# x1 of the next sample ahead of the end of an older norm on VectorE, in a chain of conditioned residual layers

## The chip, the cores and the metric

The kernel runs on one core of one Trainium2 chip. The metric is the device time of the whole program in microseconds (us). Before the change three runs took 1144.47, 1144.3 and 1142.27 us; the median is 1144.3.

The engines are called as in the profile: PE is TensorE's matmuls and PEld its weight loads, DVE is VectorE, ACT is ScalarE, POOL is GpSimd, SP is the engine that issues most DMAs.

## What is computed

The input x holds 128 samples of 128 rows by 512 features, fp32. Each sample runs through four residual layers, each with weights or factors that belong to a category of that sample:

```python
def reference(x, itok_B_0_7, condB_deltat, itok_B_0_63, itok_B_0_8, ...):
    # layer 0: W = weight[subject_id]; y = einsum('bnh,boh->bno', x, W) + bias[subject_id]
    x = x + _L0_cond_ref(x, itok_B_0_7, L0_cond_weight, L0_cond_bias)
    # layer 1: pairs of rows are rotated and scaled by angles and amplitudes ** delta_t
    x = x + _L1_cond_ref(x, condB_deltat, L1_cond_amplitudes, L1_cond_frequencies)
    # layer 2: einsum('bsd,bdh->bsh', x, W[cat_ids]) + b[cat_ids]
    x = x + _L2_cond_ref(x, itok_B_0_63, L2_cond_W, L2_cond_b)
    # layer 3: adapter (512 -> 128 -> relu -> 512), added to its input, then a norm
    #   over the 512 features with gamma and beta of the sample's language
    x = x + _L3_cond_ref(x, itok_B_0_8, L3_cond_W1, ..., L3_cond_gamma, L3_cond_beta)
    return x
```

Layer 0 has 8 weight matrices for 128 samples, layer 2 has 64.

## The kernel before

The samples are handled one at a time, in an order sorted by subject, so that the weight of layer 0 (W0) changes seldom: after the first two samples at samples 30, 31, 61, 70, 89, 110 and 117. The weight of layer 2 (W2, 1 MB) is loaded anew for each sample. The residual of layers 0 and 2 is folded in by adding the identity to the diagonal blocks of the weight. The matmuls of layers 0 and 2 and the second one of the adapter run on operands split into a rounded part (hi) and its rest (lo), as hi x hi + lo x hi + hi x lo. ScalarE makes the hi parts; VectorE makes the lo parts of the weights and of x2; GpSimd makes the lo parts of x and h.

Each engine has its own program, written out by hand as a loop `for s in range(1, B)`; one pass is called a turn here. Semaphores alone tie the engines together, and each engine works through its list in order.

TensorE in turn s: the first half of layer 0 of sample s+1 (L1048, L1052), layer 2 of sample s (L1090 with x2T_hi and w_hi, L1094 with x2T_lo, L1100 with w_lo, the last two of its four matmuls waiting for the second half of w_lo), the rest of layer 0 of sample s+1 (L1059, L1064, then l0_done), the transpose of x3 (L1110), the adapter's second matmul of sample s-1 (up, L1130 to L1133, then up_done), the rotation of sample s+1 (L1075, needs x1), the adapter's first matmul of sample s (down, L1120).

VectorE in turn s, in this order: w_lo, first half (rest_of_w2, L873); x2T_lo (L890); a half or both halves of w0_lo where sample s+1 brings a new W0 (rest_of_w0, L864); w_lo, second half (L873); the mixing matrix (L845); centre of sample s-2, which subtracts the mean and multiplies by gamma (L924); x3 of sample s (finish_l2, L902, needs l2_done); the end of the norm of sample s-2 (finish_norm, L935: times rstd, plus x3_beta, into the output buffer yb); x1 of sample s+1 (finish_l0, L883: ps_l0 plus bias, needs l0_done); the first half of w0_lo where sample s+2 brings a new W0 and 18 <= s+2 < 110 (rest_of_w0, L864); the add of x3 to the adapter's result of sample s-1 (add_x3, L915, needs up_done).

GpSimd in turn s: var_eps and rstd of sample s-2 (L482, L487) after the second half of w_lo; the identity onto W2 of sample s+1 (L469); h_lo (L500); x_lo of sample s+2 (L476); x3_beta of sample s-1 (add_beta, L508); if sample s+3 brings a new W0, the identity onto it (L461) and the copy of its bias (L464).

SP in turn s issues the loads of W2 (s+3), x (s+4) and the rows per sample (s+2), then the store of sample s-2, which waits for out_made (L342), then the load of W1 (s+2), which waits for the down matmuls of turn s (L336), then perhaps a W0 (s+5).

The profile's names leave buffer numbers out: `ps_l` is ps_l0 or ps_l2, `x<-ps_l,b_sb` is x1, `x<-ps_l,rows` is x3, `x_beta` is x3_beta, `w_lo<-w_in,w_hi` is w2_lo at L873 and w0_lo at L864.

Of the kernel before, what the change touches and what calls it, by code (L numbers as in the profile page):

```python
# [18 lines left out]
def conditioned_residual_stack(  # L19
# [32 lines left out]
    with ctx:  # L52
# [199 lines left out]
        def is_first(eng, s):  # L252
            return eng.value_load(ids[0:1, bass.ds(4 * B + s, 1)], min_val=0, max_val=1)
# [12 lines left out]
        def landed(s, n):  # L266

            return 16 * (s // n + 1)
# [448 lines left out]
        def _(dve):  # L717
# [112 lines left out]
            def coefficients():  # L830

                dve.wait_ge(power_made, 4)
                dve.wait_ge(trig_made, 1)
                for n, wide in enumerate((sin_of, cos_of)):
                    dve.tensor_tensor(wide.rearrange("p (f e) -> p f e", e=2),
                                      power.unsqueeze(2).broadcast_to([P, F, 2]),
                                      trig[:, n * F:(n + 1) * F].unsqueeze(2).broadcast_to([P, F, 2]), ALU.mult)\
                        .then_inc(coef_wide, 1)

            def make_mix(s):  # L840

                if s >= 1:
                    dve.wait_ge(mix_done, s)
                dve.wait_ge(diag_made, s + 1)
                dve.scalar_tensor_tensor(out=mix[:, :], in0=signed_swap[:, :], scalar=sin1[:, s:s + 1],  # L845
                                         in1=ps_diag[:, :], op0=ALU.mult, op1=ALU.add).then_inc(mix_made, 1)
# [8 lines left out]
            def rest_of_w0(s, parts, first):  # L855

                e = s % 2
                with dve.If(first):

                    dve.wait_ge(w2_hi_made, 2 * s - 1)  # L860
                    dve.wait_ge(l0_done, s - 1)
                    for n in parts:
                        half = halves[n]
                        dve.tensor_tensor(w0_lo[e][:, half], w0_in[e][:, half], w0_hi[e][:, half].bitcast(fp32),  # L864
                                          ALU.subtract).then_inc(w0_lo_made[e], 1)

            def rest_of_w2(s, n):

                half = halves[n]
                if s >= 1:  # L870
                    dve.wait_ge(l2_done, s)
                dve.wait_ge(w2_hi_made, 2 * s + n + 1)
                dve.tensor_tensor(w2_lo[:, half], w2_in[s % WB][:, half], w2_hi[:, half].bitcast(fp32),  # L873
                                  ALU.subtract).then_inc(w2_lo_made, 1)

            def finish_l0(s):

                if s >= 1:
                    dve.wait_ge(mix_done, s)
                if s < 2:  # L880
                    dve.wait_ge(b0_loaded[s], 16)
                dve.wait_ge(l0_done, s + 1)
                dve.tensor_tensor(x1[:, :], ps_l0[:, :], b0_sb[s % 2][:, :], ALU.add).then_inc(x1_made, 1)  # L883

            def rest_of_x2T(s):

                if s >= 1:
                    dve.wait_ge(l2_done, s)
                dve.wait_ge(x2T_hi_made, s + 1)
                dve.tensor_tensor(x2T_lo[:, :], ps_mix[:, :], x2T_hi[:, :].bitcast(fp32), ALU.subtract)\  # L890
                    .then_inc(x2T_lo_made, 1)

            def finish_l2(s):

                dve.wait_ge(l2_done, s + 1)
                if s >= 2:
                    dve.wait_ge(x3beta_made, s - 1)
                if s < 2:
                    dve.tensor_copy(x3[s % X3B][:, :], ps_l2[:, :]).then_inc(x3_made, 1)
                    return  # L900
                dve.wait_ge(rows_loaded[s % RB], landed(s, RB))
                dve.tensor_tensor(x3[s % X3B][:, :], ps_l2[:, :], rows[s % RB][:, bias_of], ALU.add).then_inc(x3_made, 1)  # L902

            def rest_of_wup(n):

                dve.wait_ge(wup_hi_made, n + 1)
                dve.tensor_tensor(wup_lo[:, wup_parts[n]], wup_sb[:, wup_parts[n]],
                                  wup_hi[:, wup_parts[n]].bitcast(fp32), ALU.subtract).then_inc(wup_lo_made, 1)

            def add_x3(s):  # L910
                y = ps_y[s % 2]
                dve.wait_ge(up_done, s + 1)
                if s >= 1:
                    dve.wait_ge(mean_made, s)
                dve.scalar_tensor_tensor(out=y[:, :], in0=y[:, :], scalar=1.0, in1=x3[s % X3B][:, :],  # L915
                                         op0=ALU.mult, op1=ALU.add, accum_out=y_sum[:, :]).then_inc(y_made, 1)

            def centre(s):

                y = ps_y[s % 2]  # L920
                if s < 2:
                    dve.wait_ge(rows_loaded[s], 16)
                dve.wait_ge(squares_made, s + 1)
                dve.scalar_tensor_tensor(out=y[:, :], in0=y[:, :], scalar=neg_mean[:, 0:1],  # L924
                                         in1=rows[s % RB][:, gamma_of],
                                         op0=ALU.add, op1=ALU.mult).then_inc(scaled_made, 1)

            def finish_norm(s):

                if s >= OB:  # L930
                    dve.wait_ge(out_stored[s % OB], landed(s, OB) - 16)
                dve.wait_ge(x3beta_made, s + 1)
                dve.wait_ge(scaled_made, s + 1)
                dve.wait_ge(rstd_made, s + 1)
                dve.scalar_tensor_tensor(out=yb[s % OB][:, :], in0=ps_y[s % 2][:, :], scalar=rstd[:, 0:1],  # L935
                                         in1=x3_beta[s % 2][:, :], op0=ALU.mult, op1=ALU.add).then_inc(out_made, 1)
# [27 lines left out]
            def in_two_turns(s):  # L964

                return 18 <= s < 110

            for s in range(1, B):
                rest_of_w2(s, 0)
                rest_of_x2T(s)  # L970
                if s < LAST:
                    rest_of_w0(s + 1, (1,) if in_two_turns(s + 1) else (0, 1), first)
                rest_of_w2(s, 1)
                if s == 1:
                    coefficients()
                    rest_of_wup(0)
                    finish_l2(1)
                    dve.wait_ge(coef_sorted, 1)
                    dve.tensor_scalar(cos1[:, 2:B], ps_y[1][:, 2:B], 1.0, None, ALU.add).then_inc(coef_made, 1)
                    rest_of_wup(1)  # L980
                    finish_l0(2)
                    rest_of_wup(2)
                    dve.wait_ge(coef_made, 2)
                if s < LAST:
                    make_mix(s + 1)
                first = is_first(dve, s + 2) if s < LAST - 1 else None
                if s >= 2:
                    centre(s - 2)
                if s >= 2:
                    finish_l2(s)  # L990
                    finish_norm(s - 2)
                    if s < LAST:
                        finish_l0(s + 1)
                if in_two_turns(s + 2):
                    rest_of_w0(s + 2, (0,), first)
                add_x3(s - 1)
# [220 lines left out]
```

## Time and profile before

| | before |
|---|---|
| median of three runs | 1144.3 us |
| the profiled execution | 1143.54 us |
| its span, first to last instruction | 1141.1 us |
| mean granted TensorE clock | 0.992 of full speed |
| PE busy | 1102.6 us (97%) |
| DVE busy | 916.4 us (80%) |
| ACT busy | 778.7 us (68%) |
| POOL busy | 677.9 us (59%) |
| DMA | 353.50 MB, mean 310 GB/s |

How to read it: the span is the time in which instructions ran; the program's own time is longer by what lies around it (2.4 us here). Busy times overlap, since the engines work side by side. A busy share near 100% says that an engine bounds the kernel only if its work is also on the chain that ended last; the chain and the waits show that. In the timelines each row has the start in us from the beginning of the span, the duration in us, the engine, the line, the operation and its tiles, and how many instructions were merged; in brackets stands how long the engine was idle before it and what ended that.

### The profile page before, as it was taken

What the parts mean: (1) busy time and instruction counts of PE and PEld (TensorE: products, weight loads), DVE (VectorE), ACT (ScalarE), POOL (GpSimd) and SP (SyncE); (2) the same over time, 40 slices, a digit from 0 to 9 for tenths busy, and PEclk for the clock granted to TensorE, in tenths of its full rate; (3) what the DMA queues carried; (4) which work ended last, traced back from release to release, by engine and by line L of the source; (5) the groups of instructions that cost most, each with busy time, mean ns of one, the idle gap of its engine ahead of it and who ended that gap; (6) DMA issues with size and microseconds to landing.
All of it is one profiled execution on the core that took longest, in us unless ns stands there. A gap on an engine that the chain in (4) does not pass through costs nothing.

```text
span 1141.1 us, 28378 instructions
## 1 busy us (share of the span) xinstructions
PE 1102.6 (97%) x6046; PEld 924.0 (81%) x6046; DVE 916.4 (80%) x1373; ACT 778.7 (68%) x1824; POOL 677.9 (59%) x807
## 2 busy tenths in 40 slices
PE   4799999999999999999999999999999999999996
PEld 2588888888788888888888888887888888787885
DVE  7787787778987787778978877878877878888876
ACT  3476776767676776767767666767767767676764
POOL 5756556557755656556656556566556566565563
PEclk9899999999999999999999999999999999999999
DMA  7898979897998999799989889988998999798882
GB/s 247 307 330 302 321 284 334 315 309 277 381 338 295 322 316 315 269 351 327 333 303 361 307 275 341 323 300 308 356 310 286 342 316 356 263 369 323 312 297 70
DMA packets 97554, 353.50 MB, mean 310 GB/s; under 512 B 11870, under 2 KB 12510, under 8 KB 79932
## 3 DMA queue, kind: packets, MB, share of 16 engines
q1 hardware_dynamic: 95756, 350.39, 86.7%
q14 instruction: 162, 1.33, 0.3%
q8 instruction: 52, 0.85, 0.3%
q10 hardware_dynamic: 1584, 0.93, 0.3%
HBM read 316.94 MB, written 34.34 MB: 308 GB/s over the span
## 4 chain that ended last, share of the span: by engine, by line
PE 92%; DVE 2%; issue 2%; ACT 1%; DMA 1%; POOL 1%; DVEq 0%; SPq 0%; POOLq 0%; ACTq 0%
PE ps_mix L1075 10%; PE ps_l L1064 10%; PE ps_l L1100 10%; PE ps_l L1048 10%; PE ps_l L1094 10%; PE ps_l L1090 10%; PE ps_hT L1120 9%; PE ps_l L1059 5%; PE ps_x3T L1110 5%; PE ps_l L1052 5%; PE ps_y L1133 3%; PE ps_y L1131 3%; PE ps_y L1130 3%; DVE w_lo L873 1%; DMA x_in<-xT 1%
## 5 line engine op out<-in xcount | busy, mean ns | idle before, releaser
L595 ACT ACTIVATE w_hi<-w_in 128x1024 fp32r<-128x1024 f32 x256 | 270.8, 1058 | 219.5 <-POOL w_in L469 219.5
L873 DVE TENSOR_TENSOR w_lo<-w_in,w_hi 128x1024 fp32r<-128x1024 f32 x256 | 333.7, 1303 | 19.8 <-ACT w_hi L595 18.1
L482 POOL TENSOR_SCALAR var_eps<-square_sum 128x1 f32<-128x1 f32 x128 | 24.4, 191 | 414.5 <-DVE w_lo L873 307.9
L902 DVE TENSOR_TENSOR x<-ps_l,rows 128x512 f32<-128x512 f32 x126 | 87.0, 691 | 124.3 <-PE ps_l L1100 124.3
L640 ACT ACTIVATE x3T<-ps_x3T,minus_bup 128x128 f32<-128x128 f32 x512 | 145.8, 366 | 49.3 <-PE ps_x3T L1110 48.0
L508 POOL TENSOR_TENSOR x_beta<-x,rows 128x512 f32<-128x512 f32 x128 | 168.8, 1319 | 0.0
L476 POOL TENSOR_TENSOR x_lo<-x_in,x_hi 128x512 fp32r<-128x512 f32 x127 | 164.1, 1292 | 7.5 <-ACT x_hi L571 7.5
L469 POOL TENSOR_TENSOR w_in<-w_in,ident 128x512 f32<-128x512 f32 x128 | 166.5, 1301 | 2.9 <-DMA w_in<-W 2.9
L1075 PEld LDWEIGHTS ps_mix<-mix,x 128*128 128x128 f32 x1024 | 125.0, 192 | 32.9 <-issue 32.8
L1048 PE MATMUL ps_l<-w_hi,x_hi 128*128 128x512 f32 x512 | 150.2, 415 | 0.0
L1075 PE MATMUL ps_mix<-mix,x 128*128 128x128 f32 x1024 | 141.9, 282 | 4.9 <-DVE x L883 4.9
L1100 PE MATMUL ps_l<-w_lo,x2T_hi 128*128 128x512 f32 x512 | 138.9, 391 | 5.7 <-DVE w_lo L873 5.7
L1090 PE MATMUL ps_l<-w_hi,x2T_hi 128*128 128x512 f32 x512 | 139.4, 394 | 0.2 <-ACT w_hi L595 0.2
L1094 PE MATMUL ps_l<-w_hi,x2T_lo 128*128 128x512 f32 x512 | 138.3, 393 | 0.3 <-DVE x2T_lo L890 0.3
L1064 PE MATMUL ps_l<-w_lo,x_hi 128*128 128x512 f32 x512 | 137.4, 391 | 0.0
L1120 PE MATMUL ps_hT<-x3T,w_in 128*128 128x128 f32 x1024 | 135.4, 276 | 0.0
L915 DVE SCALAR_TENSOR_TENSOR ps_y<-ps_y,x 128x512 f32<-128x512 f32 x128 | 89.5, 699 | 47.6 <-PE ps_y L1133 47.6
L1120 PEld LDWEIGHTS ps_hT<-x3T,w_in 128*128 128x128 f32 x1024 | 124.8, 192 | 0.4 <-issue 0.4
L1100 PEld LDWEIGHTS ps_l<-w_lo,x2T_hi 128*128 128x128 f32 x512 | 95.8, 188 | 28.3 <-DVE w_lo L873 8.8
L1090 PEld LDWEIGHTS ps_l<-w_hi,x2T_hi 128*128 128x128 f32 x512 | 96.7, 189 | 22.6 <-issue 1.5
L1094 PEld LDWEIGHTS ps_l<-w_hi,x2T_lo 128*128 128x128 f32 x512 | 96.4, 189 | 22.1 <-DVE x2T_lo L890 2.3
L1064 PEld LDWEIGHTS ps_l<-w_lo,x_hi 128*128 128x128 f32 x512 | 96.2, 188 | 20.0
(148 smaller groups left out, 1843.7 us busy)
## 6 DMA issues: line engine op xcount, KB each, us to landing
w_in<-W SPq DMA_DIRECT2D x128, 1024.0 KB, 6.6
rows<-sample_rows SPq DMA_DIRECT2D x128, 768.0 KB, 7.1
x_in<-xT SPq DMA_DIRECT2D x128, 256.0 KB, 6.2
w_in<-W SPq DMA_DIRECT2D x128, 256.0 KB, 5.0
out<-yb SPq DMA_DIRECT2D x128, 256.0 KB, 6.6
w_in<-W0T SPq DMA_DIRECT2D x7, 1024.0 KB, 5.5
wup_sb<-Wup SPq DMA_DIRECT2D x1, 2560.0 KB, 13.7
w_in<-W0T SPq DMA_DIRECT2D x4, 512.0 KB, 6.4
```

Of the source, the lines that this page charges most:

```text
L469: pool.tensor_tensor(diagonal_of(w2_in[s % WB]), diagonal_of(w2_in[s % WB]), ident[:, :].unsqueeze(1).broadcast_to([P, C, P]), ALU.add).th ...
L476: pool.tensor_tensor(x_lo[s % 2][:, :], x_in[s % XB][:, :], x_hi[s % 2][:, :].bitcast(fp32), ALU.subtract).then_inc(x_lo_made, 1)
L508: pool.tensor_tensor(x3_beta[s % 2][:, :], x3[s % X3B][:, :], rows[s % RB][:, beta_of], ALU.add)\
L595: act.activation(w2_hi[:, halves[n]], w2_in[s % WB][:, halves[n]], ACT.Copy).then_inc(w2_hi_made, 1)
L873: dve.tensor_tensor(w2_lo[:, half], w2_in[s % WB][:, half], w2_hi[:, half].bitcast(fp32), ALU.subtract).then_inc(w2_lo_made, 1)
L1048: pe.matmul(ps_l0[:, :], x_hi[s % 2][:, c * N:(c + 1) * N], w0_hi[s % 2][:, c * D:(c + 1) * D], start=(c == 0), stop=False)
L1064: mm = pe.matmul(ps_l0[:, :], x_hi[s % 2][:, c * N:(c + 1) * N], w0_lo[s % 2][:, c * D:(c + 1) * D], start=False, stop=(c == C - 1))
L1075: mm = pe.matmul(ps_mix[:, c * N:(c + 1) * N], x1[:, c * P:(c + 1) * P], mix[:, :], start=True, stop=True)
L1090: pe.matmul(ps_l2[:, :], x2T_hi[:, c * N:(c + 1) * N], w2_hi[:, c * D:(c + 1) * D], start=(s >= 2 and c == 0), stop=False)
L1094: mm = pe.matmul(ps_l2[:, :], x2T_lo[:, c * N:(c + 1) * N], w2_hi[:, c * D:(c + 1) * D], start=False, stop=False)
L1100: mm = pe.matmul(ps_l2[:, :], x2T_hi[:, c * N:(c + 1) * N], w2_lo[:, c * D:(c + 1) * D], start=False, stop=(c == C - 1))
L1120: mm = pe.matmul(ps_hT[:, :], w1_in[s % 2][:, c * A:(c + 1) * A], x3T[:, c * N:(c + 1) * N], start=(c == 0), stop=(c == C - 1))
```

## The change

In VectorE's turn, finish_l0(s + 1) is moved ahead of finish_norm(s - 2). The two operations themselves, their waits and all other programs stay as they are. The order x3, end of norm, x1 becomes x3, x1, end of norm. It concerns turns 2 to 126. The rows per sample (bias, gamma and beta in one load) and rstd first on GpSimd belong to the kernel before already.

```diff
@@ -988,9 +988,9 @@
                     centre(s - 2)
                 if s >= 2:
                     finish_l2(s)
-                    finish_norm(s - 2)
                     if s < LAST:
                         finish_l0(s + 1)
+                    finish_norm(s - 2)
                 if in_two_turns(s + 2):
                     rest_of_w0(s + 2, (0,), first)
                 add_x3(s - 1)
```

## Rows read from the trace of the kernel before

**Rows 1.** The page: the chain that ended last, shares of the span by engine
```profile
PE 92%; DVE 2%; issue 2%; ACT 1%; DMA 1%; POOL 1%; DVEq 0%; SPq 0%; POOLq 0%; ACTq 0%
```
**Rows 2.** Waits, whole span: engine line waited for, us in total, times, longest us
```profile
PE ps_mix L1075 <- DVE x L883: 4.9, 3, 3.7
```
**Rows 3.** Timeline of an ordinary turn: start us, us, engine, line, operation
```profile
607.95 1.07 PE L1064 MATMUL ps_l<-w_lo,x_hi 128*128 128x512 f32 x4
608.31 0.74 DVE L935 SCALAR_TENSOR_TENSOR yb<-ps_y,rstd,x_beta 128x512 f32<-128x512 f32 x1
...
609.13 0.69 DVE L883 TENSOR_TENSOR x<-ps_l,b_sb 128x512 f32<-128x512 f32 x1
...
610.20 0.70 DVE L915 SCALAR_TENSOR_TENSOR ps_y<-ps_y,x 128x512 f32<-128x512 f32 x1 [0.38 <-PE ps_y L1133]
...
610.82 1.22 DVE L873 TENSOR_TENSOR w_lo<-w_in,w_hi 128x1024 fp32r<-128x1024 f32 x1
...
611.96 0.68 DVE L890 TENSOR_TENSOR x2T_lo<-ps_mix,x2T_hi 128x512 fp32r<-128x512 f32 x1
...
612.85 1.23 DVE L873 TENSOR_TENSOR w_lo<-w_in,w_hi 128x1024 fp32r<-128x1024 f32 x1 [0.21 <-ACT w_hi L595]
...
614.13 1.07 PE L1094 MATMUL ps_l<-w_hi,x2T_lo 128*128 128x512 f32 x4
```
**Rows 4.** Timeline of the turn after a late TensorE (turn 88)
```profile
796.43 0.73 DVE L935 SCALAR_TENSOR_TENSOR yb<-ps_y,rstd,x_beta 128x512 f32<-128x512 f32 x1
796.56 1.08 PE L1064 MATMUL ps_l<-w_lo,x_hi 128*128 128x512 f32 x4
...
797.75 0.69 DVE L883 TENSOR_TENSOR x<-ps_l,b_sb 128x512 f32<-128x512 f32 x1 [0.58 <-PE ps_l L1064]
```
**Rows 5.** Timeline: x1 and SP's store and W1 load in an ordinary turn
```profile
848.35 0.69 DVE L883 TENSOR_TENSOR x<-ps_l,b_sb 128x512 f32<-128x512 f32 x1
...
848.83 0.35 SPq L342 DMA_DIRECT2D out<-yb  x1
...
851.38 0.33 SPq L336 DMA_DIRECT2D w_in<-W  x1
```
**Rows 6.** Timeline, turns 59 and 60, sample 61's W0; last row: turn 87, sample 89
```profile
548.59 1.28 POOL L476 TENSOR_TENSOR x_lo<-x_in,x_hi 128x512 fp32r<-128x512 f32 x1
...
549.33 1.63 DVE L864 TENSOR_TENSOR w_lo<-w_in,w_hi 128x1024 fp32r<-128x1024 f32 x1
...
549.83 2.27 POOL L508 TENSOR_TENSOR x_beta<-x,rows 128x512 f32<-128x512 f32 x1
...
551.49 1.70 DVE L873 TENSOR_TENSOR w_lo<-w_in,w_hi 128x1024 fp32r<-128x1024 f32 x1
...
556.10 0.73 PE L1100 MATMUL ps_l<-w_lo,x2T_hi 128*128 128x512 f32 x2 [0.60 <-DVE w_lo L873]
...
788.76 2.28 POOL L508 TENSOR_TENSOR x_beta<-x,rows 128x512 f32<-128x512 f32 x1
```
**Rows 7.** Timeline, turns 28 and 29: the W0 of sample 30, before sample 31's
```profile
284.42 2.29 POOL L508 TENSOR_TENSOR x_beta<-x,rows 128x512 f32<-128x512 f32 x1
286.67 2.28 POOL L461 TENSOR_TENSOR w_in<-w_in,ident 128x512 f32<-128x512 f32 x1
288.89 1.61 POOL L464 COPY b_sb<-b_in 128x512 f32<-128x512 f32 x1
...
289.95 1.62 DVE L873 TENSOR_TENSOR w_lo<-w_in,w_hi 128x1024 fp32r<-128x1024 f32 x1
```
**Rows 8.** Timeline, turn 29: the first half of the W0 of sample 31
```profile
294.03 0.69 DVE L883 TENSOR_TENSOR x<-ps_l,b_sb 128x512 f32<-128x512 f32 x1 [0.27 <-PE ps_l L1064]
294.94 1.62 DVE L864 TENSOR_TENSOR w_lo<-w_in,w_hi 128x1024 fp32r<-128x1024 f32 x1 [0.22 <-ACT w_hi L595]
...
295.43 2.28 POOL L508 TENSOR_TENSOR x_beta<-x,rows 128x512 f32<-128x512 f32 x1
```
**Rows 9.** Timeline, turn 109: the first w_lo ahead of sample 110's W0
```profile
968.09 1.88 DVE L873 TENSOR_TENSOR w_lo<-w_in,w_hi 128x1024 fp32r<-128x1024 f32 x1
```

## The prediction, made before the change was run

> **What bounds the kernel now.** I read the page first: the chain that ended last is TensorE for 92% of the span [rows 1]. So an edit on VectorE is worth only what it takes from, or adds to, TensorE's waits. The second view is the list of waits: in the whole run TensorE's matmuls waited on x1 (L883) three times, 4.9 us together, 3.7 of them once [rows 2]; that long one belongs to the start, which the change does not touch. The third view is the timeline of one ordinary turn [rows 3]. Its reader should compare two ends: the last L1064 matmul of the next sample ends at 607.95+1.07 = 609.02, the norm on VectorE at 608.31+0.74 = 609.05, and x1 starts at 609.13. Which of the two released x1? One turn decides it: there the norm ended at 796.43+0.73 = 797.16, the matmuls at 796.56+1.08 = 797.64, and x1 started at 797.75, 0.11 after the matmuls, the same 0.11 as in the ordinary turn, though the norm had been done for 0.59 us [rows 4]. So x1 already starts as early as TensorE lets it; the norm in front of it fills a gap in which VectorE has nothing else.
>
> I also use a spacing: VectorE starts an operation 0.08 us before the recorded end of the one ahead if nothing else holds it (L873 at 610.82 takes 1.22, L890 follows at 611.96, 1.14 later) [rows 3]. A norm of 0.74 thus moves what is behind it by 0.66.
>
> **x1 ahead of the norm, ordinary turns.** 125 turns are changed (s = 2 to 126); in 120 no half of a W0 stands between the norm and the add of x3. There x1 keeps its start (gain 0). VectorE stands idle where the norm was, at x1's wait for l0_done; the norm, the add of x3 and the first w_lo are queued behind it. The norm then starts at 609.13+0.61 = 609.74, the add at 610.40 instead of 610.20, w_lo at 611.02 instead of 610.82, x2T_lo at 612.16 instead of 611.96 [rows 3]. The second w_lo could follow at 612.76, but it was waiting for ScalarE's w_hi until 612.85 anyway, so it does not move. x2T_lo ends at 612.84 and its user L1094 starts at 614.13: 1.29 us of cover [rows 3]. So 120 x 0 = 0. If the ScalarE cover were gone, the 0.2 would still end in the idle time that VectorE has before the next x3.
>
> Who waits for the norm's result: its store on SP; rstd, add_beta and the matmuls of up, all of them a turn later. SP: x1 at 848.35 in that turn means a norm that ends about 849.7, 0.9 later than the store was issued (848.83); behind the store stands only the load of W1, issued 2.55 us later at 851.38, after a wait for the down matmuls. One SP load with its register work takes about 1.2, so 0.9+1.2 fits into 2.55 [rows 5]. Cost 0; the store's bytes move by 1 us.
>
> **The five turns with half a W0 in front of the add.** Where sample s+2 brings a new W0 (samples 30, 31, 61, 70, 89), the first half of its w0_lo (L864) stands between x1 and the add. Here nothing absorbs: from x1 to the second w_lo VectorE has no gap and TensorE waits at its end (0.60 us in the turn shown) [rows 6]. The norm now lies inside this chain, and there is a second effect. L864 and L873 and GpSimd's adds and subtractions exclude each other: L864 at 549.33 took 1.63, because x_lo on GpSimd ran until 549.87, and 549.87+1.08 = 550.96 is its end; then L508, begun at 549.83, took 2.27, until 1.14 after L864; then L873, at 551.49, took 1.70 and ended 1.09 after L508 [rows 6]. Alone L873 takes 1.22 [rows 3].
> With the change, L864 asks at 549.33+0.66 = 549.99, and now L508 (549.83) is ahead of it by 0.16. So: L508 549.83 to 551.10 (1.27), L864 ends 551.10+1.08 = 552.18, the add starts 552.10, L873 at 552.71, now free of GpSimd, and ends 553.92 (1.21) instead of 553.19. That is +0.73, and it goes unchanged through x2T_lo, the other half and the second w_lo to TensorE's L1100 at 556.10. The turns for samples 70 and 89 repeat these rows (of the last of the three its L508 stands there, 788.76 with 2.28): 3 x 0.73 = 2.19.
>
> The turn for sample 30 has two more GpSimd operations behind, as sample 31 brings a W0 as well. Same steps [rows 7]: L508 284.42 to 285.70; L864 to 286.78; L461 to 287.93 (1.15 behind it, as L461 was before: 286.67+2.28); L873 waits for it, ends 289.01; x2T_lo 288.93; the copy L464, which needs about 0.5 free of VectorE, ends 289.48; the second half 289.53 to 290.74; the second w_lo 290.67 to 291.88, where it was 289.95+1.62 = 291.57. +0.31.
>
> The turn for sample 31: L864 started at 294.94 after a wait for ScalarE and was held by x_lo until 295.48. x1 at 294.03 gives an order-bound request at 294.03+0.62+0.66 = 295.31, still before L508 at 295.43 and inside x_lo. So its end does not move: 0; if L508 gets ahead, 0.73 [rows 8]. I take 0, with 0.12 us to spare.
>
> Samples 110 and 117 have both halves behind x2T_lo. There L873 (968.09) was held by L508 until 968.89, and a request 0.2 later is held until the same moment: 0 [rows 9].
>
> Here a rule was weighed. The rows show exclusion by whole instructions, won by whoever asked first [rows 6]. The Trainium skill, SBUF — State Buffer, section "Who interferes with whom", says the same of a VectorE instruction with two SBUF inputs against a GpSimd one that reads SBUF: the first to issue holds the port, the other is blocked. By that rule the order 549.83 before 549.99 decides; were the ports shared by bandwidth instead, the norm's 0.66 alone would count. No run here shows an order turned round by the change yet.
>
> **Sum.** 2.19+0.31+0 = 2.5 us. The profiled execution took 1143.5 (span 1141.1, 2.4 around it), so 1146.0. The median of the runs is 1144.3, 0.8 above that execution; on it the sum is 1146.8. I give the middle, 1146.4.
>
> **Rivals.**
> 1. The lock falls to VectorE (this one is not slower beyond what can be told). If L864's request came 0.16 earlier or L508's later, L864 would run 549.99 to 551.20, L508 to 552.34, L873 to 553.42: +0.23 instead of +0.73. Four turns: +0.9, time 1144.8. For it: 0.16 us is little. Against: the three like turns repeat each other closely. It decides from the moment that the norm, from x1, is over before L508 is begun. 14%.
> 2. The lock falls to GpSimd in the turn for sample 31 as well: 2.5+0.73 = 3.2, time 1147.1. 12%.
> 3. x1 was held by the norm's end after all (0.08 before it). Then it starts up to 0.08 earlier in 125 turns, up to 10 us: down to 1136. Against it stand rows 4. 5%.
> 4. The 0.2 us of the ordinary turn reaches TensorE: 120 x 0.2 = 24, time 1170, or a part of that. It decides where the cover of x2T_lo falls below 0.2; it is 1.29 now. 4%.
> 5. The order changes and nothing else does (delays of VectorE are paid back somewhere I did not see): 1143.9. 7%.
> The forecast: 58%.
>
> **How the numbers follow.** A difference under 0.2% (2.3 us) can't be told from none here. The forecast of 2.5 lies just above it, and the three runs before differ by 2.2, so of its 58 I put 35 to slower and 23 to same. Rival 2 gives 11 to slower, 1 to same; rival 4 gives 4 to slower; rivals 1 and 5 go to same (21). Slower 0.50, same 0.45, faster 0.05. The range: down to the middle between rivals 1 and 5 less a little for the runs, 1143.7; up to rival 2 with 0.9 for the runs, 1148.0. It leaves out rivals 3 and 4 and the tails.
>
> **What would show it.** In an ordinary turn x1 0.11 after the L1064 group, the norm 0.61 behind x1, the add about 0.2 later, the second w_lo and the turn's length unchanged. In the turns for samples 61, 70 and 89: L508 at about 1.27, L864 at about 2.2, the next L873 at about 1.22, and TensorE's wait at L1100 longer by 0.73 (0.60 to 1.33). For 31, L864 still about 1.25 and its end where it was. Wrong if x1 comes earlier than 0.11 after the matmuls, if L864 is about 1.2 and L508 about 2.4, or if SP's W1 load slips.

## The result, and the profile after

| | before | after |
|---|---|---|
| median of 7 runs each, in turn on one chip | 1144.47 us (1142.27 to 1146.38) | 1147.55 us (1146.78 to 1149.08) |
| the profiled execution | 1143.54 us | 1148.48 us |
| its span | 1141.1 us | 1146.5 us |
| mean granted TensorE clock | 0.992 | 0.989 |
| PE busy / DVE busy | 1102.6 / 916.4 us | 1104.5 / 901.5 us |

The ratio is 1.0029, with a 95% interval from 1.0020 to 1.0038: the kernel became slower by 0.29%, about 3.3 us. Forecast were 1146.4 us and +2.5. The two profiled spans differ by 5.4 us. Of these 1.94 lie ahead of the place where the new order begins (the x1 of sample 3 starts at 64.02 before and at 65.96 after), and they are not the change's: the eight kernels below have that x1 anywhere from 61.55 to 65.47. From there to the x1 of sample 127 it is 1057.40 before and 1060.85 after, +3.45. The lower mean clock of after is no cause either: from 64 to 1120 us the granted clock is 1.00 in both traces, and what is missing ahead of it (0.74 against 0.66 from 20 to 40 us, 0.93 against 0.86 from 40 to 64) belongs to the start.

The page, chain that ended last, shares by engine; it answers to [rows 1]:
```profile
PE 91%; DVE 3%; issue 2%; DMA 1%; ACT 1%; POOL 1%; DVEq 0%; SPq 0%; POOLq 0%; ACTq 0%
```
VectorE has one point more and TensorE one less. Then the list of waits (engine, line waited for, us in total, times, longest us), first of before:
```profile
DVE ps_y L915 <- PE ps_y L1133: 47.6, 121, 2.2
...
DVE w_lo L873 <- ACT w_hi L595: 18.1, 81, 0.9
...
DVE x L883 <- PE ps_l L1064: 3.2, 9, 0.6
...
PE ps_l L1094 <- DVE x2T_lo L890: 0.3, 1, 0.3
```
and of after, with the line that answers to [rows 2]:
```profile
DVE x L883 <- PE ps_l L1064: 95.1, 126, 1.1
...
PE ps_mix L1075 <- DVE x L883: 5.9, 3, 4.8
...
PE ps_l L1094 <- DVE x2T_lo L890: 4.1, 5, 1.6
...
DVE ps_y L915 <- PE ps_y L1133: 3.0, 2, 2.2
...
DVE w_lo L873 <- ACT w_hi L595: 1.6, 4, 0.9
```
This is the change in one view. VectorE now stands at x1 in all 126 turns (95.1 us, 0.74 in the ordinary one), and two waits that it had behind x1, for TensorE's L1133 and for ScalarE's w_hi, are nearly gone (47.6 and 18.1 us). The idle time moved; it did not shrink. For the time only the waits of PE count. There L1094's wait for x2T_lo grew, from 0.3 to 4.1 us. The other line that grew, L1075, did so by its one long wait (4.8 for 3.7), which lies in the start.

An ordinary turn of after, to be laid on [rows 3] by the start of x1:
```profile
612.04 1.07 PE L1064 MATMUL ps_l<-w_lo,x_hi 128*128 128x512 f32 x4
...
613.22 0.69 DVE L883 TENSOR_TENSOR x<-ps_l,b_sb 128x512 f32<-128x512 f32 x1 [0.74 <-PE ps_l L1064]
...
613.83 0.74 DVE L935 SCALAR_TENSOR_TENSOR yb<-ps_y,rstd,x_beta 128x512 f32<-128x512 f32 x1
...
614.49 0.69 DVE L915 SCALAR_TENSOR_TENSOR ps_y<-ps_y,x 128x512 f32<-128x512 f32 x1
...
616.23 0.68 DVE L890 TENSOR_TENSOR x2T_lo<-ps_mix,x2T_hi 128x512 fp32r<-128x512 f32 x1
...
616.94 1.23 DVE L873 TENSOR_TENSOR w_lo<-w_in,w_hi 128x1024 fp32r<-128x1024 f32 x1
...
617.98 0.87 PEld L1094 LDWEIGHTS ps_l<-w_hi,x2T_lo 128*128 128x128 f32 x4
...
618.20 1.07 PE L1094 MATMUL ps_l<-w_hi,x2T_lo 128*128 128x512 f32 x4
```
x1 starts at 613.22, 0.11 after the L1064 group (612.04+1.07 = 613.11), as before. The norm follows 0.61 behind it. The add stands 1.27 behind x1 (before 1.07), x2T_lo 3.01 (before 2.83), the second w_lo 3.72 in both, L1094 4.98 (before 5.00). The next x1 starts at 621.65, so the turn takes 8.43.

Turns 59 and 60 of after, with the W0 of sample 61; they answer to [rows 6]:
```profile
552.00 0.69 DVE L883 TENSOR_TENSOR x<-ps_l,b_sb 128x512 f32<-128x512 f32 x1 [0.74 <-PE ps_l L1064]
...
552.61 0.74 DVE L935 SCALAR_TENSOR_TENSOR yb<-ps_y,rstd,x_beta 128x512 f32<-128x512 f32 x1
...
553.15 1.26 POOL L508 TENSOR_TENSOR x_beta<-x,rows 128x512 f32<-128x512 f32 x1
553.27 2.22 DVE L864 TENSOR_TENSOR w_lo<-w_in,w_hi 128x1024 fp32r<-128x1024 f32 x1
...
556.02 1.21 DVE L873 TENSOR_TENSOR w_lo<-w_in,w_hi 128x1024 fp32r<-128x1024 f32 x1
...
557.89 1.20 PE L1094 MATMUL ps_l<-w_hi,x2T_lo 128*128 128x512 f32 x4 [0.75 <-DVE x2T_lo L890]
...
558.89 1.21 DVE L873 TENSOR_TENSOR w_lo<-w_in,w_hi 128x1024 fp32r<-128x1024 f32 x1
...
560.16 0.73 PE L1100 MATMUL ps_l<-w_lo,x2T_hi 128*128 128x512 f32 x2 [0.62 <-DVE w_lo L873]
```
L508 now stands in front of L864 (553.15 before 553.27) and is no longer blocked: 1.26 for 2.27. L864 pays for it, 2.22 for 1.63. The second w_lo ends at 560.10, 8.10 behind x1. TensorE waits 0.75+0.62 = 1.37 in this turn, where it waited 0.60. In the traces of before and after, 93 of 98 lengthened w_lo operations of VectorE ended 1.07 to 1.09 after the end of the GpSimd operation that had begun before them (here 553.15+1.26 = 554.41 and 553.27+2.22 = 555.49), and each of the ten lengthened additions and subtractions of GpSimd 1.13 to 1.16 after VectorE's end.

The table that the rest goes by: from the start of one x1 to the next, in us, for the samples that bring a new W0, and the sum of all other turns (samples 4 to 127 without these seven).

| | 30 | 31 | 61 | 70 | 89 | 110 | 117 | sum | others |
|---|---|---|---|---|---|---|---|---|---|
| before | 10.75 | 10.10 | 9.80 | 9.80 | 10.11 | 10.00 | 9.68 | 70.23 | 987.17 |
| after | 11.44 | 10.30 | 10.56 | 10.53 | 10.56 | 10.05 | 9.96 | 73.41 | 987.45 |

The 117 other turns are the same within 0.3 us. The loss is where a W0 is made, but not in each of these columns: what 31, 89 and 117 hold besides the change is told below.

### The profile page after: what moved, and what is told of

Its sections match the earlier page's. It is cut to its first block, busy times and chain, and to the rows that moved or that the text cites. A ratio compares the mean times of both kernels' runs of the same rounds, so it can differ in the third digit from the quotient of the medians.

```text
span 1146.5 us, 28378 instructions
## 1 busy us (share of the span) xinstructions
PE 1104.5 (96%) x6046; PEld 925.0 (81%) x6046; DVE 901.5 (79%) x1373; ACT 782.0 (68%) x1824; POOL 673.6 (59%) x807
## 3 DMA queue, kind: packets, MB, share of 16 engines
q14 instruction: 162, 1.33, 0.3%
## 4 chain that ended last, share of the span: by engine, by line
PE 91%; DVE 3%; issue 2%; DMA 1%; ACT 1%; POOL 1%; DVEq 0%; SPq 0%; POOLq 0%; ACTq 0%
PE ps_mix L1075 10%; PE ps_l L1064 10%; PE ps_l L1100 10%; PE ps_l L1090 10%; PE ps_l L1048 10%; PE ps_l L1094 10%; PE ps_hT L1120 9%; PE ps_l L1059 5%; PE ps_l L1052 5%; PE ps_x3T L1110 5%; PE ps_y L1133 2%; PE ps_y L1131 2%; PE ps_y L1130 2%; DVE w_lo L864 1%; DMA x_in<-xT 1%
## 5 line engine op out<-in xcount | busy, mean ns | idle before, releaser
L873 DVE TENSOR_TENSOR w_lo<-w_in,w_hi 128x1024 fp32r<-128x1024 f32 x256 | 328.7, 1284 | 3.8 <-ACT w_hi L595 1.6
L902 DVE TENSOR_TENSOR x<-ps_l,rows 128x512 f32<-128x512 f32 x126 | 87.1, 691 | 118.3 <-PE ps_l L1100 118.3
L508 POOL TENSOR_TENSOR x_beta<-x,rows 128x512 f32<-128x512 f32 x128 | 164.8, 1288 | 0.0
L883 DVE TENSOR_TENSOR x<-ps_l,b_sb 128x512 f32<-128x512 f32 x128 | 88.6, 692 | 95.1 <-PE ps_l L1064 95.1
L1075 PEld LDWEIGHTS ps_mix<-mix,x 128*128 128x128 f32 x1024 | 125.7, 193 | 34.1 <-issue 34.0
L1075 PE MATMUL ps_mix<-mix,x 128*128 128x128 f32 x1024 | 142.7, 283 | 5.9 <-DVE x L883 5.9
L1100 PE MATMUL ps_l<-w_lo,x2T_hi 128*128 128x512 f32 x512 | 139.5, 392 | 5.2 <-DVE w_lo L873 5.2
L1094 PE MATMUL ps_l<-w_hi,x2T_lo 128*128 128x512 f32 x512 | 138.3, 392 | 4.1 <-DVE x2T_lo L890 4.1
L1064 PE MATMUL ps_l<-w_lo,x_hi 128*128 128x512 f32 x512 | 137.4, 390 | 0.0
L1100 PEld LDWEIGHTS ps_l<-w_lo,x2T_hi 128*128 128x128 f32 x512 | 96.1, 189 | 27.9 <-DVE w_lo L873 8.2
L1094 PEld LDWEIGHTS ps_l<-w_hi,x2T_lo 128*128 128x128 f32 x512 | 96.3, 189 | 26.2 <-DVE x2T_lo L890 6.2
L1064 PEld LDWEIGHTS ps_l<-w_lo,x_hi 128*128 128x128 f32 x512 | 96.1, 188 | 20.1
```

The lines of the kernel that those rows point to most:

```text
L508: pool.tensor_tensor(x3_beta[s % 2][:, :], x3[s % X3B][:, :], rows[s % RB][:, beta_of], ALU.add)\
L1064: mm = pe.matmul(ps_l0[:, :], x_hi[s % 2][:, c * N:(c + 1) * N], w0_lo[s % 2][:, c * D:(c + 1) * D], start=False, stop=(c == C - 1))
L1075: mm = pe.matmul(ps_mix[:, c * N:(c + 1) * N], x1[:, c * P:(c + 1) * P], mix[:, :], start=True, stop=True)
L1094: mm = pe.matmul(ps_l2[:, :], x2T_lo[:, c * N:(c + 1) * N], w2_hi[:, c * D:(c + 1) * D], start=False, stop=False)
L1100: mm = pe.matmul(ps_l2[:, :], x2T_hi[:, c * N:(c + 1) * N], w2_lo[:, c * D:(c + 1) * D], start=False, stop=(c == C - 1))
```

## The experiments

All have the time of the kernel before from the same chip, measured in turn with them. Line numbers from the first edited line on are shifted in some of them; the tiles stay the same.

### The old order in five turns, and the new order in these five alone

```diff
# e1, against after; e2 has the two branches exchanged
-                    if s < LAST:
+                    if s in (28, 29, 59, 68, 87):
+                        finish_norm(s - 2)
                         finish_l0(s + 1)
-                    finish_norm(s - 2)
+                    else:
+                        if s < LAST:
+                            finish_l0(s + 1)
+                        finish_norm(s - 2)
```


> The changed order everywhere but in the five turns (28, 29, 59, 68, 87) that have half of a W0 ahead of the add. Theory A (the whole loss sits in these turns, the ordinary ones hide the norm): ratio to before 1.000, within 0.1%. Theory B (the ordinary turns or the store order pay part of it): the ratio stays between 1.001 and 1.003.

> The changed order in the five turns alone. Theory A: the whole loss, 2.5 to 3.3 us, ratio 1.0022 to 1.003; L508 ahead of L864 in turns 28, 59, 68 and 87, and TensorE's wait for x2T_lo and w_lo 0.7 us longer in each. Theory B: less than half of it.

| | median us | of before | ratio, 95% | W0 30, 31, 61, 70, 89 | others |
|---|---|---|---|---|---|
| e1: old order in the five | 1146.63 | 1145.62 | 1.0008 (0.9996 to 1.0020) | 10.89, 10.06, 9.85, 9.78, 9.92 | 988.88 |
| e2: new order in the five | 1148.53 | 1145.62 | 1.0031 (1.0019 to 1.0043) | 11.49, 10.09, 10.56, 10.60, 10.56 | 987.18 |

(The ratios are the record's estimates; the plain quotients of the medians beside them are 1.0009 and 1.0025.) The loss comes with the five turns: e2, with the old order in 120 turns, is as slow as the changed kernel, and e1, with the new order in 120, can't be told from the kernel before. By the interval of e1 alone the 120 ordinary turns could still cost up to 2.3 us. That they do not is shown by the traces: 987.17 for the 117 other turns before and 987.45 after. The 1.7 us of "others" by which e1 differs is told at the end.

### The norm behind the half of W0, and the add of beta behind the add of x3

By the forecast's rival 1, only a third of the 0.73 would be left if L864 kept the port; the rest is the order on the port. Two kernels take that order away in different ways. The first puts the norm behind the half of W0, so that L864 asks before L508:

```diff
# e3, against after
-                    finish_norm(s - 2)
                 if in_two_turns(s + 2):
                     rest_of_w0(s + 2, (0,), first)
+                if s >= 2:
+                    finish_norm(s - 2)
                 add_x3(s - 1)
```


> x1, then the half of W0 where there is one, then the norm, then the add. Lock theory: L864 asks before L508 again, so L508 is held until L864 ends and the first w_lo, 0.66 later than before the change, finds L508 just done: the second w_lo ends 0.16 later than before the change, some 0.6 us in all, ratio 1.0005. Delay theory (only the 0.66 of the norm on the chain counts, the lock does not): 4 x 0.66 = 2.6 us, ratio 1.0023.

The second leaves VectorE as after, and holds GpSimd's L508 back in the five turns until the add of x3 is done:

```diff
# e4, against after, in GpSimd's turn ahead of add_beta
+                if s in (28, 29, 59, 68, 87):
+                    pool.wait_ge(y_made, s)
```


> The changed kernel, but in the five turns GpSimd's x3_beta (L508) waits until the add of x3 is done, so it can't hold the port against L864. Lock theory: L864 takes 1.21 instead of 2.2; L508 then meets the second half of W0 behind x2T_lo and holds that back 0.5; from x1 to the end of the second w_lo 7.6 us, where it was 7.34 before the change and 8.10 after; in all about 1 us over before, ratio 1.001. Delay theory: no shorter than after, 8.1 us, ratio 1.0025.

| | median us | of before | ratio, 95% | W0 30, 31, 61, 70, 89 |
|---|---|---|---|---|
| e3: norm behind the half | 1146.30 | 1145.62 | 1.0011 (1.0001 to 1.0021) | 10.95, 10.24, 10.11, 10.02, 9.97 |
| e4: add of beta later | 1148.64 | 1145.62 | 1.0031 (1.0019 to 1.0043) | 12.42, 10.06, 10.06, 10.07, 10.06 |

Timeline of e3, turn 59:
```profile
550.27 0.69 DVE L883 TENSOR_TENSOR x<-ps_l,b_sb 128x512 f32<-128x512 f32 x1 [0.74 <-PE ps_l L1065]
...
551.02 1.62 DVE L864 TENSOR_TENSOR w_lo<-w_in,w_hi 128x1024 fp32r<-128x1024 f32 x1
...
551.51 2.28 POOL L508 TENSOR_TENSOR x_beta<-x,rows 128x512 f32<-128x512 f32 x1
...
552.57 0.74 DVE L935 SCALAR_TENSOR_TENSOR yb<-ps_y,rstd,x_beta 128x512 f32<-128x512 f32 x1
...
553.83 1.21 DVE L873 TENSOR_TENSOR w_lo<-w_in,w_hi 128x1024 fp32r<-128x1024 f32 x1
```
L864 has the port first again (551.02 before 551.51), and L508 takes 2.28 as in [rows 6]. The norm now fills the time in which L873 would have stood behind L508: L873 takes 1.21 where it took 1.70. The second w_lo ends 7.64 behind x1, for 7.34 before and 8.10 after; in turns 68 and 87 it ends at 7.55 and 7.51, near the 0.16 that I had expected. So x1 in front of the norm costs 0.16 to 0.30 in such a turn, not 0.76, if the norm isn't in front of the half of W0. The ratio, 1.0011 (1.0001 to 1.0021), agrees with that and excludes the 1.0023 of a delay without a port.

Timeline of e4, turn 59, then turn 28 with the TensorE rows at its end:
```profile
551.40 0.69 DVE L885 TENSOR_TENSOR x<-ps_l,b_sb 128x512 f32<-128x512 f32 x1 [0.74 <-PE ps_l L1066]
...
552.66 1.22 DVE L866 TENSOR_TENSOR w_lo<-w_in,w_hi 128x1024 fp32r<-128x1024 f32 x1
...
554.63 2.16 POOL L508 TENSOR_TENSOR x_beta<-x,rows 128x512 f32<-128x512 f32 x1 [2.08 <-DVE ps_y L917]
...
557.80 1.21 DVE L875 TENSOR_TENSOR w_lo<-w_in,w_hi 128x1024 fp32r<-128x1024 f32 x1
...
289.25 2.25 POOL L461 TENSOR_TENSOR w_in<-w_in,ident 128x512 f32<-128x512 f32 x1
...
290.30 2.28 DVE L875 TENSOR_TENSOR w_lo<-w_in,w_hi 128x1024 fp32r<-128x1024 f32 x1
...
292.63 0.80 PE L1102 MATMUL ps_l<-w_lo,x2T_hi 128*128 128x512 f32 x2 [2.16 <-DVE w_lo L875]
...
294.30 1.91 PE L1066 MATMUL ps_l<-w_lo,x_hi 128*128 128x512 f32 x4
```
In turn 59 the norm stands in front of L866 as in after, nothing is on the port, and L866 takes 1.22. The second w_lo ends at 559.01, 7.61 behind x1: +0.27 against before. The samples 61 and 70 take 10.06, +0.26, instead of +0.76 and +0.73.

The 0.76 can now be added up from the time that VectorE's operations stand blocked. The norm puts 0.66 into the chain in each case. Before, L864 and L873 are blocked for 0.42+0.49 = 0.91. In after L864 is blocked for 1.01 and nothing else: 0.66+1.01-0.91 = 0.76. In e4 only the second half of W0 is blocked, by the L508 that was moved there, for 0.52: 0.66+0.52-0.91 = 0.27. In e3 only L864, for 0.41: 0.16, and in the turn shown L864 starts 0.13 later behind x1 besides. So 0.5 to 0.6 of the 0.76 goes when L508 is not in front of L864, whichever of the two ways is taken.

In turn 28 the same edit pushed L461 into the second w_lo (2.28 us), and sample 30 took 12.42, +1.67. My expectation had not followed what stands behind L508 on GpSimd. But the port made only a small part of this: from x1 to the end of the second w_lo the turn takes 8.68, for 8.29 before and 8.97 after. The rest is TensorE's clock. TensorE had waited 2.16 us at L1102; between 294 and 296 us the granted clock was 0.50 (the level of 1.2 GHz), and the L1066 group (L1064 in the kernel before) took 1.91 for 1.08, and L1061 (L1059) 1.22 for 0.72. That is 1.3 of the 1.67. No other trace has such a stretch in this turn; after 64 us and up to 1120 us only e6 has one more, in the turn for sample 110, behind a wait of 1.74. The five turns together are +2.1 in e4 and +2.8 in after. That the total stayed at 1.0031 is thus made of a gain at the port, a loss by the clock and the longer ordinary turns told at the end, as far as one trace can say.

### How far the cover of the ordinary turn reaches

The forecast gave 120 x 0 on the strength of 1.29 us of cover behind x2T_lo. Two kernels put extra work at the norm's place in all changed turns but the five: the norm's second operation once or twice more, into spare tiles that nobody reads.

```diff
# e5, against after; e6 has range(2)
+        spare = [sb(f"spare{i}", [N, D]) for i in range(1)]
...
+                for copy in (spare if twice else ()):
+                    dve.scalar_tensor_tensor(out=copy[:, :], in0=ps_y[s % 2][:, :], scalar=rstd[:, 0:1],
+                                             in1=x3_beta[s % 2][:, :], op0=ALU.mult, op1=ALU.add)
...
-                    finish_norm(s - 2)
+                    finish_norm(s - 2, s not in (28, 29, 59, 68, 87))
```


> The changed kernel; in all turns but the five, a second operation of the norm's kind (same inputs, into a spare tile) stands ahead of the norm: 0.66 us more on VectorE behind x1, 120 times. Cover theory (x2T_lo has 1.29 us before TensorE needs it, of which the change spends 0.2 at most): ordinary turns stay at 8.43 to 8.45, same time as the changed kernel, ratio to before 1.003. Rival (the ordinary turn is near its edge): each turn grows, by up to 0.66, 8 to 80 us more.

> Two such operations, 1.32 us more per ordinary turn. Cover theory: x2T_lo now ends at 614.16 on the scale of rows 3, 0.03 after its user's 614.13, so L1094 starts 0.05 behind it: 0.08 per turn, some 10 us, ratio 1.012; PE's L1094 waits for x2T_lo in every ordinary turn. Rival (cover larger than read): 0.

e5: 1147.17 us for 1144.15 of before, 1.0036 (1.0023 to 1.0049). e6: 1179.14 us, 1.0313 (1.0293 to 1.0332). With one more operation nearly all ordinary turns keep 8.42 to 8.46, though VectorE is 0.66 later in each; the turns that end in the x1 of samples 29, 60, 69, 88, 109 and 116, each just ahead of a new W0, and one more (50) grew, to 8.76 to 8.81, and two (16 and 40) to 8.57 and 8.56. The turns of samples 30, 61, 70 and 89, behind four of them, are in turn 0.3 to 0.5 shorter than in after (10.13 for 10.56 at 61). With two more operations, the ordinary turn takes 8.64 to 8.70. The cover is real and it ends between the two, but sooner than I had worked out for e6. Timeline of e5, an ordinary turn, then of e6:
```profile
600.27 0.69 DVE L884 TENSOR_TENSOR x<-ps_l,b_sb 128x512 f32<-128x512 f32 x1 [0.74 <-PE ps_l L1068]
...
605.02 0.87 PEld L1098 LDWEIGHTS ps_l<-w_hi,x2T_lo 128*128 128x128 f32 x4
...
605.25 1.07 PE L1098 MATMUL ps_l<-w_hi,x2T_lo 128*128 128x512 f32 x4
```
```profile
599.64 0.69 DVE L884 TENSOR_TENSOR x<-ps_l,b_sb 128x512 f32<-128x512 f32 x1 [0.77 <-PE ps_l L1068]
...
603.97 0.69 DVE L891 TENSOR_TENSOR x2T_lo<-ps_mix,x2T_hi 128x512 fp32r<-128x512 f32 x1
...
604.71 0.75 PEld L1098 LDWEIGHTS ps_l<-w_hi,x2T_lo 128*128 128x128 f32 x4 [0.33 <-DVE x2T_lo L891]
604.71 1.19 PE L1098 MATMUL ps_l<-w_hi,x2T_lo 128*128 128x512 f32 x4
```
What needs x2T_lo first is not the matmul but its weight load, which starts 4.75 behind x1 where nothing holds it, 0.23 ahead of the matmul. In e6 x2T_lo ends at 604.66, 5.02 behind x1; the load follows at 5.07, 0.32 late, load and matmul are recorded as starting together, and the group ends 6.26 behind x1 instead of 6.05: +0.21, and the turn grew by 0.21 to 0.26. I had set the end of x2T_lo against the matmul's start, which lets 0.22 too much count as cover. In the changed kernel the cover is thus 617.98 less 616.91 = 1.07 us, not 1.29.

### The half of W0 ahead of x3

If the half of W0 behind x1 is what makes these turns long, it may be moved to a place where VectorE stands idle: ahead of x3 (L902), where it waits for TensorE 118.3 us in the changed kernel. Both kernels do so in the five turns, one with the old order and one with the new.

```diff
# e7, against before; e8 has x1 ahead of the norm besides
+                if in_two_turns(s + 2):
+                    first_half_of_w0(s + 2, first)   # waits for w0_rounded, which ScalarE raises after the half
                 if s >= 2:
                     finish_l2(s)
                     finish_norm(s - 2)
                     if s < LAST:
                         finish_l0(s + 1)
-                if in_two_turns(s + 2):
-                    rest_of_w0(s + 2, (0,), first)
```


> The order before the change (norm ahead of x1), but the first half of a two-turn W0 (L864) is moved ahead of x3, into the idle time that VectorE has there; it waits on a semaphore of its own for the rounded half. x3 starts 0.7 later in those turns, x1 0.5 later (the norm is in front of it and x3 late), TensorE's rotation 0.5 later; the chain from x1 to the second w_lo loses 1.6 us and no longer stops TensorE. The five turns pairs take 8.9 instead of 9.8 to 10.7: some 5 us faster than before, ratio 0.996.

> The same with x1 ahead of the norm. Here x3 is late, so the norm would be in front of x1 while TensorE has its matmuls done: x1 is 0.25 earlier than in the other kernel, held by TensorE again. Pairs take 8.7: about 1 us faster than with the old order, some 6 us faster than before, ratio 0.995. If the order doesn't matter here either, both are equal within 0.1%.

e7: 1144.32 us, 1.0003 (0.9994 to 1.0012). e8: 1144.24 us, 1.0000 (0.9991 to 1.0009). Both are as fast as the kernel before, and neither faster, against my expectation (0.996 and 0.995). Without a half of W0 behind x1, the order of x1 and the norm makes no difference that can be measured; that part held. Where the gain went, the timeline of e7, turn 59, shows:
```profile
548.48 1.23 DVE L875 TENSOR_TENSOR w_lo<-w_in,w_hi 128x1024 fp32r<-128x1024 f32 x1
...
548.57 2.27 POOL L471 TENSOR_TENSOR w_in<-w_in,ident 128x512 f32<-128x512 f32 x1
...
550.80 0.46 POOL L502 TENSOR_TENSOR h_lo<-h,h_hi 128x128 fp32r<-128x128 f32 x1
...
552.46 1.27 POOL L510 TENSOR_TENSOR x_beta<-x,rows 128x512 f32<-128x512 f32 x1
...
552.47 2.34 DVE L884 TENSOR_TENSOR w_lo<-w_in,w_hi 128x1024 fp32r<-128x1024 f32 x1
```
The half (L875) now blocks the identity (L471, 2.27 instead of 1.29), which makes h_lo late, for which TensorE's weight load of L1144 then waits 0.21 us; and L510, late as well, is in front of L884 by 0.01 us and blocks it (2.34). Sample 61 comes down from 9.80 to 9.26, and the turn ahead of it goes up from 8.43 to 8.94: 18.20 for 18.23. The blocking on the port has moved to other operations and has not gone.

This pair also shows what x1 held by the norm looks like, and that even this costs nothing here. In e7 the late x3 pushes the norm back, and the x1 of sample 60 starts at 550.88, right behind the norm and 0.61 behind the end of TensorE's L1075 group, which is L1064 in the kernel before (549.20+1.07 = 550.27). In e8 it starts 0.10 behind that group; the turn ahead keeps 8.42, sample 61 takes 9.78, and the sum is 18.20 again.

## Why the prediction was right

The range (1143.7 to 1148.0) held 1147.55, the case with the largest chance (slower) came, and its mechanism was there. Step by step:

- **x1 is held by TensorE, not by the norm: right.** It starts 0.10 to 0.12 behind the L1064 group in every turn from sample 4 on but one, and in the ordinary turn with 0.74 of idle time ahead. Rival 3 (1136) is out.
- **Ordinary turns 120 x 0: right.** e2 shows it by the total, e1 within its interval, the 117 other turns by 987.17 against 987.45. The add is 0.20 later, as worked out, and the second w_lo does not move. The reason given for the cover was a little off: 1.07, up to the weight load, not 1.29, up to the matmul. e5 and e6 bracket it. Rival 4 (1170) is out; e6 shows what it would look like.
- **Samples 61, 70, 89, each +0.73: right.** +0.76, +0.73 and +0.45. In the kernel before, the last one had a gap of 0.23 in TensorE's own issue ahead of L1059, which makes the late turn of [rows 4]. Ahead of that gap the difference is there: the second w_lo ends 8.10 behind x1 for 7.35, +0.75. L508 at 1.26 and L864 at 2.22 are as written. Only the place of TensorE's wait was wrong: not all at L1100 (1.33), but 0.75 at L1094 and 0.62 at L1100.
- **Who gets the port: right.** 553.15 before 553.27, and L508 is 0.12 to 0.16 ahead in three turns of three; in turn 28 it is 0.04 ahead. The Trainium skill, SBUF — State Buffer, section "Who interferes with whom", says that the first to issue holds the port and the other is blocked; this case now agrees with an order turned round by a change (L508 1.26 for 2.27, L864 2.22 for 1.63). Rival 1 (+0.23, L864 in front) did not come; e3, which makes L864 ask first, and e4, which holds L508 back, show its size in turn 59, +0.30 and +0.27.
- **Sample 31, 0: right.** There L864 starts at 298.40 and L508 at 298.53, 0.13 apart for 0.12 forecast, so rival 2 is out. From x1 to the end of the second w_lo it is 7.63 in both kernels. The 0.20 more of the table comes behind that, where TensorE's L1059 starts 0.13 late, with nothing that the trace shows to wait for.
- **Sample 30, +0.31: too small; it was +0.69.** This term was mis-sized. Turn 28 of after, answering to [rows 7]:
```profile
285.69 0.69 DVE L883 TENSOR_TENSOR x<-ps_l,b_sb 128x512 f32<-128x512 f32 x1 [0.74 <-PE ps_l L1064]
...
286.92 1.26 POOL L508 TENSOR_TENSOR x_beta<-x,rows 128x512 f32<-128x512 f32 x1
286.96 2.31 DVE L864 TENSOR_TENSOR w_lo<-w_in,w_hi 128x1024 fp32r<-128x1024 f32 x1
...
289.43 1.28 POOL L461 TENSOR_TENSOR w_in<-w_in,ident 128x512 f32<-128x512 f32 x1 [1.25 <-DMA b_in<-b]
...
289.80 2.00 DVE L873 TENSOR_TENSOR w_lo<-w_in,w_hi 128x1024 fp32r<-128x1024 f32 x1
```
  I had L461 follow L508 at once, held by L864 until 1.15 behind it, so that it would end 4.65 behind x1. It ended at 5.02, 0.37 later, and L873 (asked at 289.80) was held until 1.09 behind that. That is the missing 0.38. Of it 0.08 is a later end of L864 (3.58 behind x1 for 3.50). The other 0.29 is the wait for the bias, a load that the chain left out: GpSimd was free 2.49 behind x1, the load was issued at 281.8 and landed 7.5 us later, 3.6 behind x1, and L461 started at 3.74, when L864 was done already. In the kernel before, the load was issued at 279.7 and landed 6.6 us later, 3.0 behind x1. At that time it would have delayed nothing in after, since L864 holds L461 until later anyway. So the step that failed is that L461 needs only GpSimd and the port. Whether the later landing belongs to the change is not shown: from issue to landing this load takes 6.6, 7.7 and 7.4 us in three kernels with the old order in turn 28 (before, e1, e7) and 7.5, 7.5 and 6.6 in three with the new one (after, e2, e4).
- **110 and 117, 0: right.** +0.05 for 110. The +0.28 of 117 is no loss: before, the x1 of sample 116 came 0.35 late for another reason (told at the end), and its w_lo operations were less late behind it; the turns of 116 and 117 together take 18.47 before and 18.39 after.
- **SP: right.** The load of W1 is issued 3.04 behind x1 in turn 59, for 3.03 in [rows 5].

The sum of what the rows ascribe to the change is 0.76+0.73+0.75+0.69 = 2.9 us, for 2.5 forecast; 0.3 of it is the late bias. By the runs it is 3.3, with an interval from 2.3 to 4.3. That the median came within 1.2 us of the forecast is in part luck, since ordinary turns alone can differ by 1.7 us between kernels for a reason that is not known, as the end of this document tells.

## What to carry to other kernels

Moving an operation to where its engine is idle anyway costs nothing and brings nothing: look first at what released the operation that is to come earlier, here TensorE and not the neighbour in the queue. The price of such an exchange sits in the few turns where the queue behind it has no gap. There it depends on the order in which two engines ask for the port that they share: the same 0.66 us of norm cost 0.76 with GpSimd's L508 in front of L864 and 0.16 to 0.30 without it. Write down both requests with their times before deciding. Measure cover up to the weight load, not up to the matmul. Follow what stands behind a blocked operation on its own engine, with the loads that it needs. After an experiment, look at the granted clock behind each long wait of TensorE, before the difference is put down to the edit.

## What the runs showed that I had not expected

**An ordinary turn has one of two lengths.** On average it takes 8.434 us in before, e2 and e3 and 8.436 in after, but 8.449 in e1 and e4. Over the 117 other turns that is 1.7 us: 987.17 before, 987.18 in e2 and 987.17 in e3, but 988.88 in e1 and e4. It does not follow the order in these turns, which is the same in after, e1, e3 and e4, and the medians of e2 and e4 are 0.1 us apart. It is half of the effect looked for. What chooses between the two stays open, and there is one trace of each kernel only.

**One late start of VectorE.** In after, the x1 of sample 5 started 0.48 behind the L1064 group instead of 0.11, though TensorE was on time:
```profile
81.67 1.07 PE L1064 MATMUL ps_l<-w_lo,x_hi 128*128 128x512 f32 x4
...
83.22 0.69 DVE L883 TENSOR_TENSOR x<-ps_l,b_sb 128x512 f32<-128x512 f32 x1 [1.12 <-PE ps_l L1064]
```
Nine of the ten traces have exactly one x1 that starts 0.46 to 0.49 behind that group with VectorE idle: at sample 5 in after, e1, e3, e4 and e8, at 116 in before and e2, at 50 in e5 and at 81 in e7. Its place is not random, then: it is 116 in both kernels that keep the old order in the ordinary turns and the rest of the program, and 5 in all four that are the changed kernel there. The cause stays open. It matters for the sums: at sample 5 it costs the whole turn 0.39, while at 116 it is made good in the next turn. A comparison of two single traces by their spans would have given 5.4 us here, where the runs say 3.3.
